# Local and sliding attention: the stack of a head pair gets four buffers instead of three

## The reference, cut to what matters

```python
# local attention: window 128, scores of a band only
band = (j > i) | (i - j > WINDOW)
scores = jnp.einsum('blhd,bmhd->bhlm', q, k) * scale + bias      # bias: lowest float in the band's outside
attn = jax.nn.softmax(scores, axis=-1)
ctx = jnp.einsum('bhlm,bmhd->blhd', attn, v).reshape(B, L, D)
...
# sliding attention: window 64, in blocks of 64
valid = (idx_raw[:, None, :, None] >= 0) & (kpos <= qpos) & (qpos - kpos < WIN)
scores = jnp.where(valid[None, None], scores, -1000000000.0)
p = jax.nn.softmax(scores.reshape(B, Hn, nb, BS, nw1 * BS), axis=-1)
out = jnp.einsum('bhnqwk,bhnwkd->bhnqd', p, vg)
```

## Time and profile before

| what | value |
|---|---|
| median of 3 runs | 3020.46 us (3018.09 to 3022.84) |
| profiled execution, its own time | 3023.02 us |
| its span, first to last instruction | 3021.2 us |
| local attention, over the heads | about 411 to 572 us of the span |
| sliding attention, over the heads | about 937 to 1082 us of the span |
| mean granted TensorE clock | 0.914 of 2.4 GHz |

### The profile page before, as it was taken

The page is one execution under the profiler, slowest core; times in us unless marked ns, Lnnn a source line. Parts: engine busy times, 40 slices in busy tenths (PEclk is TensorE's granted clock), DMA queues, the critical chain, the costliest instruction groups (busy, mean ns, idle before and its releaser), DMA issues. The chain is left out here.

```text
span 3021.2 us, 48788 instructions
## 1 busy us (share of the span) xinstructions
PE 2605.4 (86%) x18006; PEld 1292.0 (43%) x18006; DVE 2228.3 (74%) x5400; ACT 1519.9 (50%) x1907; POOL 333.1 (11%) x610
## 2 busy tenths in 40 slices
PE   6699748789994757999999997993899999999799
PEld 3588624478872431222222214882121222221588
DVE  6644577444456757999999974557899999997554
ACT  2222234432222431777777785222177777778422
POOL 4100131110002130000000001004000000000100
PEclk8799969889996875999999998996599999999899
DMA  2000042000004212100111100001211011110000
GB/s 55 22 23 14 7 117 55 2 22 16 21 8 127 46 59 58 22 18 16 23 23 23 23 2 11 22 16 64 53 23 23 13 21 23 23 23 2 16 21 25
DMA packets 62282, 88.95 MB, mean 29 GB/s; under 512 B 13927, under 2 KB 39405, under 8 KB 62077
## 3 DMA queue, kind: packets, MB, share of 16 engines
q1 hardware_dynamic: 60028, 84.04, 11.1%
q10 hardware_dynamic: 512, 1.57, 0.2%
q0 software_dynamic: 1536, 0.63, 0.1%
HBM read 57.93 MB, written 26.22 MB: 28 GB/s over the span
## 5 line engine op out<-in xcount | busy, mean ns | idle before, releaser
L1062 DVE TENSOR_REDUCE pair_mx<-ps 128x1 f32<-128x512 f32 x2048 | 1270.9, 683 | 39.4 <-PE ps L904 34.9
L1034 ACT ACTIVATE prob<-ps 128x1024 f32<-128x1024 f32 x1024 | 990.1, 1021 | 250.0 <-PE ps L939 248.3
L904 PE MATMUL ps<-k_stack,q_stack 48*128 48x512 bf16 x2048 | 643.5, 405 | 89.7 <-DMA k_stack<-image_dram 47.6
L904 PEld LDWEIGHTS ps<-k_stack,q_stack 48*128 48x128 bf16 x2048 | 148.5, 93 | 937.8 <-DVE pair_mx L1062 844.9
L953 PE MATMUL ps<-prob,v_head 128*32 128x512 f32 x4096 | 547.6, 607 | 1.3 <-ACT prob L1034 1.0
L1741 DVE TENSOR_TENSOR hid<-silu,ps 128x512 f32<-128x512 f32 x360 | 246.1, 685 | 370.0 <-PE ps L1678 251.0
L1710 ACT ACTIVATE silu<-ps 128x512 f32<-128x512 f32 x360 | 214.5, 597 | 575.1 <-PE ps L1678 567.1
L939 PE MATMUL ps<-q_stack,k_stack 51*128 51x512 bf16 x2048 | 438.6, 383 | 8.5 <-ACT prob L1034 5.3
L1690 PEld LDWEIGHTS ps<-wd,hid 128*128 128x128 f32 (+1 forms) x2880 | 364.3, 191 | 27.7 <-issue 2.7
L1690 PE MATMUL ps<-wd,hid 128*128 128x128 f32 (+1 forms) x2880 | 368.9, 275 | 0.8 <-DVE hid L1741 0.3
L1678 PE MATMUL ps<-ht_part,wg_part 128*128 128x512 f32 (+1 forms) x1080 | 335.9, 420 | 16.8 <-PEq L299 14.8
(11 more groups left out here) (186 smaller groups left out, 1798.2 us busy)
## 6 DMA issues: line engine op xcount, KB each, us to landing
q_stack<-image_dram SPq DMA_DIRECT2D x92, 192.0 KB, 4.5
k_stack<-image_dram SPq DMA_DIRECT2D x92, 192.0 KB, 4.7
image_dram<-parts SPq DMA_DIRECT2D x16, 768.0 KB, 4.3
image_dram<-parts SPq DMA_DIRECT2D x16, 512.0 KB, 5.3
image_dram<-parts SPq DMA_DIRECT2D x16, 256.0 KB, 5.1
wg<-in_L_ffn_Wg_dram SPq DMA_DIRECT2D x18, 176.0 KB, 2.4
wu<-in_L_ffn_Wu_dram SPq DMA_DIRECT2D x18, 176.0 KB, 2.5
wd<-in_L_ffn_Wd_dram SPq DMA_DIRECT2D x18, 128.0 KB, 2.4
```

The source lines that it names most:

```text
L904: nc.tensor.matmul(max_bank(n), rows_of(c.q_stack, b, g, ROWS, slice(t * P, (t + 1) * P)), rows_of(c.k_stack, b, g, ROWS, slice(k * CHUNK, ...
L1034: nc.scalar.activation(c.prob[:, u % P_UNITS, :], c.ps[:, 2 * (u % 2) * CHUNK:2 * (u % 2) * CHUNK + UNIT], ACT.Exp, scale=scale).then_inc( ...
L1062: nc.vector.reduce_max(mx[:, w:w + 1], max_bank(n), AX.X).then_inc(max_taken.sem, 1)
```

## The change

The number of stack buffers in the two windowed attentions becomes four (`PAIR_STACKS`), in the buffer's index, in the semaphores, in SP's wait before a load and in the allocation. Full attention keeps three. The memsets of `k_stack` rows (L807) cover all buffers and grow with them; they are not in the diff, as their code is the same.

```diff
 STACKS = 3
+PAIR_STACKS = 4
...
     def max_units(pe, h, w):
 
-        b = h % STACKS
+        b = h % PAIR_STACKS
         if w == 0:
-            pe.wait_ge(*stack_loaded[b].after((h // STACKS + 1) * LOADS * 16))
+            pe.wait_ge(*stack_loaded[b].after((h // PAIR_STACKS + 1) * LOADS * 16))
...
             def load_stacks(h):
 
-                if h >= STACKS:
-                    sp.wait_ge(*st_ready.after((h - STACKS + 1) * EXP_UNITS))
+                if h >= PAIR_STACKS:
+                    sp.wait_ge(*st_ready.after((h - PAIR_STACKS + 1) * EXP_UNITS))
                 for g in range(2):
                     load_half(sp, h, g)
 
             load_half(sp, 0, 0)
-            for h in range(1, STACKS):
+            for h in range(1, PAIR_STACKS):
                 load_stacks(h)
             for e in range(PAIRS):
                 sp.wait_ge(*rows_taken.after(e + 1))
                 store_shift(sp, e, 0)
-                if 1 <= e < PAIRS - STACKS + 1:
-                    load_stacks(e + STACKS - 1)
+                if 1 <= e < PAIRS - PAIR_STACKS + 1:
+                    load_stacks(e + PAIR_STACKS - 1)
...
-                               ("parts", [P, 2, PARTS, N_TOK], bf16), ("k_stack", [P, STACKS, N_TOK], bf16),
-                               ("q_stack", [P, STACKS, N_TOK], bf16), ("v", [P, TILES, D], fp32),
+                               ("parts", [P, 2, PARTS, N_TOK], bf16), ("k_stack", [P, PAIR_STACKS if paired else STACKS, N_TOK], bf16),
+                               ("q_stack", [P, PAIR_STACKS if paired else STACKS, N_TOK], bf16), ("v", [P, TILES, D], fp32),
```

More of the change, by code:

```diff
@@ L1123, in window_heads_stage @@
     nc = c.nc
-    stack_loaded = [c.count(f"full_stack_loaded_{b}") for b in range(STACKS)]
+    stack_loaded = [c.count(f"full_stack_loaded_{b}") for b in range(PAIR_STACKS)]
     v_staged = c.count("full_v_staged")
@@ L1231, in exp_unit @@
         unit = e * EXP_UNITS + u
-        b = e % STACKS
+        b = e % PAIR_STACKS
         if u == SHIFT_UNIT and e < PAIRS - 1:
@@ L1290, in store_shift @@
     def store_shift(engine, e, g):
-        dst = rows_of(c.q_stack, e % STACKS, g, EXP_ROWS, slice(0, N_TOK))[ROWS:EXP_ROWS]
+        dst = rows_of(c.q_stack, e % PAIR_STACKS, g, EXP_ROWS, slice(0, N_TOK))[ROWS:EXP_ROWS]
         engine.dma_start(dst.rearrange("s (t n) -> s t n", n=P), c.pair_rows[g * PARTS * TILES:(g + 1) * PARTS * TILES, :])\
@@ L1462, in _ @@
                 store_shift(sp, e, 0)
-                if 1 <= e < PAIRS - STACKS + 1:
-                    load_stacks(e + STACKS - 1)
+                if 1 <= e < PAIRS - PAIR_STACKS + 1:
+                    load_stacks(e + PAIR_STACKS - 1)
     biased.passed(len(biases))
-    for b in range(STACKS):
-        stack_loaded[b].passed(len(range(b, PAIRS, STACKS)) * LOADS * 16)
+    for b in range(PAIR_STACKS):
+        stack_loaded[b].passed(len(range(b, PAIRS, PAIR_STACKS)) * LOADS * 16)
     for sig, n in ((v_staged, 2 * PAIRS), (max_ready, len(place)), (max_taken, len(place)), (rowmax_ready, PAIRS),
```

## The result

The changed kernel takes 2993.5 us (median of 4 runs, 2991.6 to 2996.3) where the kernel before takes 3020.2 us: a ratio of 0.9912, interval 0.9895 to 0.9929, 26.6 us less. The prediction was 2991 us, with a range of 2983 to 3006.

The account below looks back on a forecast made before the run. The prediction took PE's waits for late stack loads, and the clock falls after most long ones, to bound the two windowed stages. Local 15.6 plus sliding 21.0 less memsets 7.1 made 29.5 us: 3020.46 to 2991 us, range 2983 to 3006.

Parts of the forecast that it names:

- The waits for the loads go: Starts of rounds 3 to 7 in local and sliding attention: PE's wait for a load becomes nothing in all ten places.
- A local round of 14.82 us: Local attention: 8.52 + 0.31 (DVE) + 0.20 (ACT's copy) + 5.79 us; five rounds take 74.1 us, 15.6 us less.
- A sliding round of 12.51 us: Sliding attention, put together from pieces at full clock; five rounds take 62.6 us in place of 83.53, 21.0 us less.
- The clock comes back: Local and sliding rounds: granted clock near 1.00 once the waits go, where it was 0.90 and 0.85.
- A: The waits go and the clock stays high in the rounds of both stages: 2991 us; chance 0.62.
- B: The waits go but the falls of the clock stay, as PE still stops for DVE and ACT: 3005.6 us; chance 0.14.
- The memsets cost 3.55 us in each projection: Longer k_stack memsets (7.11 us each) hold up DVE's second cast and the first stores; 7.1 us more over both projections.
- Rival C: The longer memsets cost nothing, since the barrier waits for something else: 2984 us; chance 0.08.
- The sum: Whole kernel: 15.6 + 21.0 - 7.1 = 29.5 us less, giving 2991 us.
- D: A part of the wait stays, one more engine being late by about 1 us at round starts: 3001 us; chance 0.11.
- E: Slower: the ten waits stay under another name and only the memsets' cost is left: 3027.6 us; chance 0.05.

Follow-up runs that it names:

- e1_old_time: Four buffers and long memsets as in the change, but SP loads a pair when it did with three; 1.0022 of the kernel before, 3028.3 us.
- e2_local_only: The change with four buffers in local attention alone, three in sliding; 0.9961 of the kernel before, 11.8 us less.
- e8_quarter_before: The kernel before, three buffers, with one short k_stack memset writing pairs of bfloat16 ones as float32; 0.9936 of the kernel before, 3002.7 us.
- e6_fill: The kernel before, three buffers, with 7 (local) or 12 (sliding) extra PE matmuls ahead of each wait for the load; 0.9951, 14.8 us less.
- e3_sliding_only: The change with four buffers in sliding attention alone, three in local; 0.9933 of the kernel before, 20.2 us less.

## Why the prediction held

**The waits for the loads go.** Right, in all ten places; `e1_old_time` shows that it is the time of the load and nothing else about the buffer.

**A local round of 14.82 us.** It is 14.83 (74.17 by five), and the same within 0.01 in all six profiles with early loads in this layer. Its two new parts were 0.31 us for DVE and 0.20 us behind ACT's copy. They measure 0.40 and, from the scores to the product, 0.38 in place of the old 0.27, so 0.11. The sum is the same, since ACT's copy ends last and PE waits for it whenever it arrives earlier: the split between the two was off by 0.09 us.

**A sliding round of 12.51 us**, put together from pieces at full clock. It is 12.49. The 0.51 us at its start was carried over from local attention and holds there too: 0.43 us for DVE (964.84), and 0.35 us from the scores to the product in place of 0.27. Not in the sum was the step from the seventh shift matmul to the eighth, which falls from 12.1 us (1051.31 to 1063.41) to 11.4 (1019.90 to 1031.28); before, the clock was still low there, 0.93 over this step. It is 0.7 us more between these two profiles alone: `e1_old_time`, `e2_local_only` and `e8_quarter_before` have the waits and take 11.4 us as well.

**The clock comes back** (A and not B). Right: 1.00 in all ten rounds. Rival B would have given 3005.6 us and a clock near 0.9. `e6_fill` shows the cause from the other side: with the waits in place and PE at work in them, the clock is 1.00 too. The stops that are left, for DVE and ACT, are at most 0.9 us and do not bring it down, against the case for B.

**The memsets cost 3.55 us in each projection.** It is 3.42 for the first store and 3.36 for the stage's end: the memset took 7.03 us where I had 7.11. Rival C is out, by these rows and by `e1_old_time` (6.6 us more for nothing gained). The exclusive lock that the page "SBUF — State Buffer" of the Trainium skill describes in the section "Who interferes with whom" agrees with every cast here: each of the 81 that start under a memset and take longer than 0.43 us ends 0.28 or 0.29 us after it, in all projections of the kernels profiled here, whatever the memset's length.

**The sum.** With the measured terms it is 15.5 + 21.1 + 0.7 - 6.8 = 30.5 us. The two measurements of the change give 26.6 and 29.0 us (0.9912 and 0.9904 of about 3022), the two profiles 31.4 and 26.1 against the profile of before. Each term is right to 1 us for the pair of profiles it was read from. But the profile of before was an unfavourable one. Five rounds with the waits took 89.68, 86.22, 86.05 and 84.88 us in four executions of local attention, and 83.53, 83.13, 83.23 and 80.59 in four of sliding attention (kernel before, `e1_old_time`, `e3_sliding_only` or `e2_local_only`, `e8_quarter_before`), with the clock lowest in the first of each. Without the waits they took 74.2 and 62.4 to 62.6 us each time. With the means of the four, 86.7 and 82.6, the gain is 12.5 + 20.2 - 6.8 = 25.9 us, at the low side of what was measured. So the prediction took the clock's part as one profile had it. It also took the 2.6 us between that execution and the median off the new kernel; as far as they were low clock in those rounds, they go with the waits and are counted twice. That its 29.5 us lie within 3 us of both measurements is in part luck: the scatter of the ratios is some 5 us either way, and the stretch after local attention alone moves by 3 us.

**D and E** did not come: DVE does have the row maximum and the turn at the start of a round, but the row maximum takes 0.18 us and DVE goes on with the next round's scores without a pause.

## What to carry to other kernels

Ask of a buffer count how many steps lie between the last reader of a buffer and the next wait for it, and compare that with one landing; here it was 4.2 us against some 6.4 for four loads in a row (470.49 to 476.86), and one more buffer put a whole round between them. Then follow everything whose size is the number of buffers, down to a memset on an engine that seems idle: what counts is not when that engine is needed but what it holds up on another. And look at the clock beside each wait of TensorE: here the waits of 2 to 3.2 us cost, by `e6_fill`, a quarter to a half of their length again in the work after them (7.0 to 14.7 us for some 27 us of waits). As that part changes from one execution to the next, take it from several profiles and not from one.

## What the runs showed of the hardware

- A cast of VectorE from float32 to bfloat16 in SBUF (0.43 us alone) waits out a running memset of GpSimd: 0.66, 1.35, 1.50, 3.05, 4.08 and 5.78 us were measured among others, each ending 0.28 or 0.29 us after the memset. Four that started in the last 0.1 us of a short memset kept their 0.43 us. The subtractions of two operands beside them stayed at 0.68 to 0.69 us under the same memsets.
- A GpSimd memset takes its time by elements in a partition, not by partitions or bytes: 5.3 us for 32 x 6144 in bfloat16 (half of 10.65), 7.0 for 32 x 8192 (half of 14.06), 6.92 for 128 x 8192, 3.51 for 128 x 4096 in float32. Writing two bfloat16 numbers as one float32 halves it.
- TensorE's clock stayed at 1.00 through five rounds in which it was busy for 64.93 of 74.17 us (local) and 52.54 of 62.44 (sliding) with waits up to 0.9 us, and stood at 0.90 and 0.85 with one wait of 2 to 3.2 us in each round. It does not fall after every such wait: the round from 466.15 in the earlier trace rows kept 1.00 with one of 2.18 us. Nor does it fall alike in every execution: four profiles with such waits have 0.90, 0.96, 0.96 and 0.98 in local attention and 0.85, 0.88, 0.88 and 0.92 in sliding attention.
- With the waits gone the rounds repeat closely: 74.16 or 74.17 us for five local rounds and 62.42 to 62.55 for five sliding ones in the six profiles with early loads in the layer, where with the waits they spread over 4.8 and 2.9 us.
